# Two 1024-column state adds a step in a selective scan, with the decay shared by ScalarE and GpSimd

## The reference

```
xr, gate = split(x @ W_in.T);  xc = silu(conv4(xr + cond));  xn = layernorm(xc)      # 512 channels
Bm, Cm, dt = split(xn @ W_xproj.T, 3)                                               # 16 each
Ad = 1 - 0.01 * tanh(dt @ W_dt.T + b_dt) * tanh(A_log)
Bd = Bm * min(norm(xn), 1)
h = clip(h * Ad[:, :, None] + Bd[:, :, None] * xn[:, None, :], -10, 10)             # each of 64 positions
y = einsum('bd,bdh->bh', Cm, h)
out = ((y + D * xn) * silu(gate)) @ W_out.T
```

## Time and profile before

| | value |
|---|---|
| median of 3 runs | 1787.09 us |
| profiled execution, its own time | 1789.41 us |
| its span (first to last instruction) | 1787.6 us |
| busy TensorE / VectorE / ScalarE / GpSimd | 1637.6 / 1613.1 / 1296.5 / 621.5 us |
| first instruction of each pass (L2014) | 743.9, 926.2, 1364.9, 1546.9 us |
| mean granted TensorE clock | 0.983 of full |

### The profile page before, as it was taken

The page is one execution under the profiler, slowest core; times in us unless marked ns, Lnnn a source line. Parts: engine busy times, 40 slices in busy tenths (PEclk is TensorE's granted clock), DMA queues, the critical chain, the costliest instruction groups (busy, mean ns, idle before and its releaser), DMA issues. The chain is left out here.

```text
span 1787.6 us, 42368 instructions
## 1 busy us (share of the span) xinstructions
PE 1637.6 (92%) x13764; PEld 703.0 (39%) x13764; DVE 1613.1 (90%) x2452; ACT 1296.5 (73%) x2197; POOL 621.5 (35%) x576
## 2 busy tenths in 40 slices
PE   7999999999999999888888889999997888888898
PEld 3555555555554455322111114444452221111144
DVE  5899999999986999889999998679998899999985
ACT  5655556455546999889999993069998899999920
POOL 0223233232331221365655560002223566555500
PEclk9999999999999999799999999999997999999999
DMA  4000000000001335544555666724445545556668
GB/s 162 2 1 0 1 2 32 2 1 0 1 1 72 139 149 177 191 163 132 182 160 188 219 189 202 239 83 157 144 159 185 179 132 183 155 189 196 189 223 288
DMA packets 126445, 226.56 MB, mean 127 GB/s; under 512 B 35617, under 2 KB 61217, under 8 KB 117537
## 3 DMA queue, kind: packets, MB, share of 16 engines
q1 hardware_dynamic: 125904, 223.30, 38.1%
q10 hardware_dynamic: 432, 1.84, 0.3%
HBM read 141.73 MB, written 83.36 MB: 126 GB/s over the span
## 5 line engine op out<-in xcount | busy, mean ns | idle before, releaser
L1038 ACT ACTIVATE R<-q,Ast 128x512 f32<-128x512 f32 x1008 | 627.0, 709 | 20.3 <-DVE q L2018 15.3
L2018 DVE CUSTOM_DVE_ANT_0 q<-R,PS 128x512 f32<-128x512 f32 x1008 | 617.3, 771 | 15.9 <-ACT R L1038 14.4
L1479 PE MATMUL PS<-xq,Uw 96*128 96x512 bf16 x1024 | 350.0, 396 | 82.3 <-DVE q L2018 71.4
L613 POOL TENSOR_TENSOR Uw<-Ub,rowmask 96x512 bf16<-96x512 bf16 x256 | 335.5, 1346 | 252.1 <-PE PS L1479 252.1
L1492 PE MATMUL PS<-q,Wy 128*32 128x512 f32 x2048 | 284.5, 618 | 0.3
L1479 PEld LDWEIGHTS PS<-xq,Uw 96*128 96x128 bf16 x1024 | 85.6, 97 | 471.1 <-DVE q L2018 399.3
L1152 PE MATMUL PS<-X,Win 128*128 (+1 forms) x456 | 214.5, 607 | 0.1
L1053 PE MATMUL PS<-xn,Wl 128*128 128x512 f32 x384 | 186.5, 609 | 0.8 <-DVE xn L1605 0.7
L1723 DVE SCALAR_TENSOR_TENSOR acc<-xp,Wc,acc 128x512 f32<-128x512 f32 x192 | 134.7, 752 | 2.6
L547 POOL TENSOR_TENSOR ex<-ex,rs 128x1024 f32<-128x1024 f32 x32 | 76.8, 2400 | 164.2 <-DVE rs L1628 164.2
L1152 PEld LDWEIGHTS PS<-X,Win 128*128 128x128 f32 x456 | 82.5, 191 | 92.5 <-issue 91.7
(11 more groups left out here) (159 smaller groups left out, 2491.9 us busy)
## 6 DMA issues: line engine op xcount, KB each, us to landing
xq<-xpart_d SPq DMA_DIRECT2D x384, 192.0 KB
sg_d<-sg SPq DMA_DIRECT2D x16, 1024.0 KB, 5.1
xn_d<-z SPq DMA_DIRECT2D x16, 1024.0 KB, 3.9
y_d<-ys SPq DMA_DIRECT2D x64, 256.0 KB, 3.9
xnp<-xn_d SPq DMA_DIRECT2D x16, 1024.0 KB, 8.4
sgp<-sg_d SPq DMA_DIRECT2D x16, 1024.0 KB, 11.5
xpart_d<-xh SPq DMA_DIRECT2D x16, 512.0 KB, 2.9
xpart_d<-xmi SPq DMA_DIRECT2D x16, 512.0 KB, 3.8
```

The costliest lines, as they stand in the source:

```text
L613: pl.tensor_tensor(Uw[0:XROWS, h, w, :, :, :], Ub[0:XROWS, w, 0:N, ds(s0, CH)].rearrange("p n t -> p t n").unsqueeze(2).broadcast_to([XROW ...
L1038: act.activation(R[:, w, :], q[:, (t + 1) % 2, w, :], ACT.Copy, scale=Ast[:, h, w, t:t + 1]).then_inc(ac_r, 1)
L1479: pe.matmul(PS[:, w, :], Uw[0:XROWS, h, w, t, :, :].rearrange("p b n -> p (b n)"), xq[0:XROWS, hb, w, s8 % XT, :], start=True, stop=True). ...
L2018: v._custom_dve(bass.dve_ops.TENSOR_ADD_SAT, out=q[:, s8 % 2, w, :], in0=R[:, w, :], in1=PS[:, w, :], s0=CLIP, s1=-CLIP).then_inc(dv_q, 1)
```

## The change

- **Two adds a step.** Groups 0 and 1 (p = 0), then 2 and 3 (p = 1) are added in one VectorE instruction of 1024 columns each, over two PSUM banks. `dv_q` counts two a step.
- **The decay is shared.** For each p, ScalarE decays the even group (512 columns) and columns 0 to 95 of the odd one (two instructions); GpSimd decays columns 96 to 511 of the odd group with a product by a broadcast column (`odd_rest`). The add of a pair waits for both (`ac_r`, and the new `pd_r`).
- **The copies of y** (`keep_y`) are moved from VectorE to ScalarE.
- **B is turned.** TensorE transposes `rB` (`turn_b`), VectorE splits it from PSUM, and SyncE stores it in 32-byte pieces into a DRAM image `bdiag_d` of the block-diagonal weights, whose zeros are written once by 12 stores during attention. `Uw` is loaded from it together with x (one more load for each two steps, 72 rows of 2 KB); GpSimd's L613, its row mask, `Ub`, its nine loads a pass and its clearing are gone. The weights have 72 rows in place of 96.
- In pass 0 the last group's middle parts are made on ScalarE, its low parts on GpSimd in halves, each between steps.

The diff, cut to its core:

```diff
+                    for b in range(2):
+                        rows = bdiag_d[ps].rearrange("(j b r) -> j b r", b=2, r=DIAG + N)[:, b, 0:DIAG]
+                        rows = rows.rearrange("j (i t w c n) -> i w c t j n", i=PARTS, t=S, w=QW, c=GB)
+                        for i in range(PARTS):
+                            sp.dma_start(rows[i, ds(w, 1), 0].rearrange("a t j n -> (a t) j n"),
+                                         tvp[b * S:(b + 1) * S, i, :].rearrange("p (j r) -> p j r", r=LANE)[:, :, 0:N]).then_inc(tv_st, 16)
...
                 def load_x(ps, k):
+                    rows = bdiag_d[ps, 0:GB * DIAG].rearrange("(r f) -> r f", f=S * ROW)
+                    sp.dma_start(Uw[0:XROWS, k % XB, :, :, :, :].rearrange("p t w b n -> p (t w b n)"),
+                                 rows[:, k * (XT * ROW):(k + 1) * (XT * ROW)].unsqueeze(0)
+                                 .broadcast_to([PARTS, GB * PARTS, XT * ROW])).then_inc(xq_in[k % XB], 16)
...
+                def odd_rest(pi, c2, s8, p):
+                    h, t = s8 // CH, s8 % CH
+                    if t < 2 and p == 0:
+                        pl.wait_ge(pl_a, pi * CHUNKS + c2 * 2 + h + 1)
+                    pl.wait_ge(dv_q, pi * (2 * S) + c2 * 16 + 2 * s8 + p + 1)
+                    alone(pl)
+                    pl.tensor_tensor(R[:, 2 * p + 1, PART:DI], q[:, (t + 1) % 2, 2 * p + 1, PART:DI],
+                                     Ast[:, h, 2 * p + 1, t:t + 1].broadcast_to([P, DI - PART]), ALU.mult).then_inc(pd_r, 1)
...
-                            for w in range(QW):
-                                act.wait_ge(dv_q, cn * (QW * CH) + QW * t + w + 1)
-                                act.activation(R[:, w, :], q[:, (t + 1) % 2, w, :], ACT.Copy,
-                                               scale=Ast[:, h, w, t:t + 1]).then_inc(ac_r, 1)
+                            for p in range(2):
+                                act.wait_ge(dv_q, cn * (2 * CH) + 2 * t + p + 1)
+                                act.activation(R[:, 2 * p, :], q[:, (t + 1) % 2, 2 * p, :], ACT.Copy,
+                                               scale=Ast[:, h, 2 * p, t:t + 1]).then_inc(ac_r, 1)
+                                act.activation(R[:, 2 * p + 1, 0:PART], q[:, (t + 1) % 2, 2 * p + 1, 0:PART], ACT.Copy,
+                                               scale=Ast[:, h, 2 * p + 1, t:t + 1]).then_inc(ac_r, 1)
+                            if t == 1 and h == 0 and before:
+                                keep_y(pi, c2 * 2 - 1, 1)
+                            if t == 1 and h == 1:
+                                keep_y(pi, c2 * 2, 0)
...
                 body(l * G + G - 2, G - 2, False)
+                pe.wait_ge(tv_s, (l * G + G - 2) * 4 + 2 + TV0)
                 for m in range(DC):
                     variance(l * G + G - 1, m, 6)
...
+                        v.wait_ge(pe_w, pi * (QW * S) + n * QW + 2 * p + 2 + W0)
+                        v.wait_ge(pe_yq, pi * (2 * S) + n * 2 - 4 + p + 1 + USED)
+                        v.wait_ge(pd_r, pi * (2 * (S - 1)) + n * 2 - 2 + p + 1 + READY)
+                        v.wait_ge(ac_r, pi * (4 * (S - 1)) + n * 4 - 4 + 2 * p + 2 + READY)
                         alone(v)
-                        v._custom_dve(bass.dve_ops.TENSOR_ADD_SAT, out=q[:, s8 % 2, w, :], in0=R[:, w, :], in1=PS[:, w, :],
+                        v._custom_dve(bass.dve_ops.TENSOR_ADD_SAT, out=state, in0=R[:, 2 * p:2 * p + 2, :].rearrange("p w c -> p (w c)"), in1=fed,
                                       s0=CLIP, s1=-CLIP).then_inc(dv_q, 1)
```

More of the change, by code:

```diff
@@ L184, in cond_resid_kernel @@
         late = ExitStack()
+        sb("table_gap", [P, TT * DI + P], where=late)
         pass_tables.append(tables(1, late))
@@ L316, in _ @@
             sp.dma_start(fold[:, :], fold_d).then_inc(ld_late, 16)
-            sp.dma_start(rowmask[:, :], rowmask_d).then_inc(ld_late, 16)
             sp.wait_ge(w_mm, G * 2)
+            sp.wait_ge(zero_r, 1)
+            for ps in range(PASSES):
+                rest = bdiag_d[ps, 0:GB * DIAG].rearrange("(p k c) -> p k c", p=P, c=1024)
+                for k in range(GB * DIAG // (P * 1024)):
+                    sp.dma_start(rest[:, k, :], words(zeros).bitcast(bf16)).then_inc(zero_in, 16)
             def load_front(n):
@@ L534, in _ @@
                 pl.memset(eps[:, n:n + 1], value).then_inc(cst, 1)
+            pl.memset(zeros[:, :], 0.0).then_inc(zero_r, 1)
             pl.wait_ge(cst, 5)
@@ new lines, in last_half, with last_group @@
+                def last_half(it, k, b):
+                    if b == 0:
+                        pl.wait_ge(xmi_r, it * TT + k + 1)
+                        alone(pl)
+                    cols = slice(b * (DI // 2), (b + 1) * (DI // 2))
+                    low = pl.tensor_tensor(xlo[:, k, cols], xr1[:, k, cols], xmi[:, k, cols], ALU.subtract)
+                    if b:
+                        low.then_inc(xlo_r, 1)
+                def last_group(n):
+                    it = l * G + G - 1
+                    if n == 20:
+                        pl.wait_ge(xq_st, it * 48 + 48)
+                        alone(pl)
+                    if 20 <= n < 20 + 2 * TT:
+                        last_half(it, (n - 20) // 2, n % 2)
@@ new lines, in eight @@
+                def eight(ps, c2, first=False, last=False, tail=False):
+                    pi = l * PASSES + ps
+                    for s8 in range(8):
+                        for p in range(2):
+                            if not (first and s8 == 0):
+                                odd_rest(pi, c2, s8, p)
+                        if tail:
+                            last_group(c2 * 8 + s8)
+                        if s8 == 0:
+                            if not first:
+                                stage_decay(ps, c2, 1)
+                        elif s8 == 1:
+                            if not first:
+                                stage_outputs(ps, c2, 1)
+                        elif s8 == 4 and not last:
+                            stage_decay(ps, c2 + 1, 0)
+                        elif s8 == 5 and not last:
+                            stage_outputs(ps, c2 + 1, 0)
+                        elif s8 == 5 and ps + 1 < PASSES:
+                            pl.wait_ge(tab_in[1], l * (16 * TABLES) + 16 * TABLES)
+                            alone(pl)
+                            stage_decay(ps + 1, 0, 0, True)
+                            stage_outputs(ps + 1, 0, 0)
+                        elif s8 == 7 and last and ps + 1 < PASSES:
+                            stage_decay(ps + 1, 0, 1, True)
+                            stage_outputs(ps + 1, 0, 1)
@@ L1025, in last_group, with last_middle, keep_y, decayed @@
                         high_part(it, 3, 7)
-                def decayed(pi, c2, first, between=None):
+                def last_middle(n):
+                    for k, at in enumerate((19, 21, 22, 23)):
+                        if n == at:
+                            middle_part(l * G + G - 1, k)
+                def keep_y(pi, ck, h):
+                    act.wait_ge(pe_yq, pi * (2 * S) + ck * (2 * CH) + 2 * CH + USED)
+                    act.wait_ge(y_out[h], pi * (CHUNKS // 2 * 16) + (ck - h) * 8 + 16)
+                    alone(act)
+                    act.activation(ys[:, h, :], PS[:, 4 + h, :], ACT.Copy).then_inc(ac_y, 1)
+                def decayed(pi, c2, first, before, between=None, after=None):
                     for h in range(2):
@@ L1465, in _, with inputs @@
                 alone(pe)
-                def inputs(pi, c2, s8, first=False):
+                def inputs(pi, c2, s8):
                     n = c2 * 8 + s8
-                    cn = pi * CHUNKS + c2 * 2 + s8 // CH
-                    h, t = s8 // CH % 2, s8 % CH
                     hb = s8 // XT % XB
@@ L1503, in _ @@
                                 last_group(c2 * 8 + s8)
-                            inputs(pi, c2, s8 + 1, ps == 0 and c2 == 0)
+                            inputs(pi, c2, s8 + 1)
                             y_of(pi, c2, s8)
@@ L2030, in eight @@
                         step(pi, c2, s8, first)
-                        if s8 == 1 and before:
-                            keep_y(pi, c2 * 2 - 1, 1)
-                        if s8 == 5:
-                            keep_y(pi, c2 * 2, 0)
                 for ps in range(PASSES):
```

261 lines of the change are left out of this document (98 added, 163 removed).

## The result

The changed kernel takes 1899.92 us (median, 1897.1 to 1902.07) against 1787.82 us of the kernel before on the same chip: a ratio of 1.0626, 95% interval [1.0606, 1.0646]. It is slower by 112 us, where 1781 us were forecast. One profiled execution further down, that of e2_three_loads, took 3036 us where its four others took 1824 to 1840, so its trace is not used.

What follows compares the result with a forecast made beforehand. VectorE's instruction rate was taken as the bound, ScalarE close behind. Steady steps +2, last group -10 and scan's start +2 gave -6 us, 1781 on the median of 1787.1; range 1762 to 1812, the forecast's own 1765 to 1783.

Steps and rivals of the forecast that it cites:

- the 204 steady steps: All scan steps but 26 in each pass 0: 2.55 us a step against 2.54, +2 us in all.
- The queue is late: Rival: B's small stores, x and weights together, 25% more bytes; a few us dearer, in the slow cases; chance 0.06.
- Up to 3 us a layer late. I take +1 for each layer in all: Scan's start: later variance matmuls and B's 32-byte stores on SyncE's queue; +1 us a layer, +2 in the sum.
- 72 rows of weights in place of 96 move the same 512 columns: nothing.: TensorE's input products in the scan: fewer rows of weights would change the time by nothing.
- As the order there is the same, it stays: TensorE's clock at the scan's start, 743.9 to 769.3 us: would stay at 0.70.
- 2.55 a step: Steady scan step: a pair's longer ring of 2.52 us plus 0.03 for disturbances, against 2.54 before.
- both rings: A pair's add, decay and hand-off back to its next add: 2.50 us through ScalarE, 2.52 through GpSimd.
- A gap of about 0.3 us before each first add: Expected VectorE profile sign: an idle gap after each two adds, ended by ScalarE's 96-column decay or by GpSimd.
- The last group, -5.1 a layer: Work slipped into pass 0's steps: -5.1 us a layer, -10 in all, with -2.5 from VectorE's 0.29 us of room.
- Adds as the bound: Rival: rings overlap more, TensorE's ring and VectorE set 2.28 us a step; 1726 us; chance 0.12.
- GpSimd's ring: Rival: product and hand-off for the odd group's 416 columns take longer, 2.67 us a step; 1807 us; chance 0.30.
- TensorE waiting for DMA at L1479's place: Profile sign that would show the forecast wrong, pointing to a late queue.

Runs made afterwards that it cites:

- e2_three_loads: The changed kernel with the weights in three loads of the same 24 rows, not one with 3 repeats outermost; 1830.14 us, ratio 1.0188.
- a1c: The changed kernel with weights loaded only for each layer's first four slots, each waited for by itself, then reused stale; 1806.87 us, ratio 1.0098.
- h1: The changed kernel with input products over 96 rows, the added rows being ones against zero weights loaded once a layer; 1895.57 us, ratio 1.0582.
- g2: The changed kernel's arithmetic (two adds, shared decay) on h3's transfers, with products over 96 rows; 1795.30 us, ratio 1.0032.
- f1: The changed kernel with one x load, three weights loads, four 512-column adds, ScalarE decaying three groups, GpSimd the fourth; 1790.96 us, ratio 1.0010.
- h2: f1 with its products over 96 rows, the added rows being ones against zero weights loaded once a layer; 1775.49 us, ratio 0.9907.
- f2: f1 with the products of x's lowest part left out, so 48 rows are loaded and multiplied; 2041.47 us, ratio 1.1408.
- h3: f2 with its products over 96 rows, 48 of them ones against zero weights; 1759.34 us, ratio 0.9818.

## Why the prediction was wrong

- **What failed: the 204 steady steps have no term for their loads, and "The queue is late ... a few us dearer, in the slow cases" was all the price they got.** The sum takes (2.55 - 2.54) x 204 = +2 us for these steps, from the engines' rings alone. But the weights' loads come with each load of x, in every second step. I took 25% more bytes as a small thing and did not ask which DMA engines the new load lies on. Measured: 43.6 and 34.2 us in the two second passes (after against a1c), 0.8 and 10.3 in the first ones, 89 in all; by the medians 93 of the 112 us. The shape of the load was there to be read beforehand, with the rule cited above: 3 repeats outermost is 48 KB on each of three engines, beside the 48 KB of x that they had in any case.
- **"Up to 3 us a layer late. I take +1 for each layer in all": not far off.** This term was for the scan's start. The first add of the first layer comes 0.9 us later than before (744.8 against 743.9), the stretch to the second layer's first add is 2.1 us longer (274.9 against 272.8).
- **What failed, smaller: "72 rows of weights in place of 96 move the same 512 columns: nothing."** Their duration is the same (0.60 us for two of them with 72 rows as with 96 in h1). But with 72 rows the first passes have less of the clock (0.86 in a1c's first one, 0.94 in g2's) and are longer: a1c against g2 is 190.5 and 184.6 against 181.9 and 180.0, 13 us together. These two differ in their loads also; f1 and h2 differ in the rows and their filling alone, and h2's first passes are 3.0 and 4.6 us shorter. While the three engines set the pace these us do not show on top (h1). "As the order there is the same, it stays", said of the clock at the start, failed with it: in the first 25.4 us of the scan the granted clock is 0.63 in the changed kernel and 0.50 in a1c, where it was 0.70.
- **2.55 a step: right; how it is made up: not quite.** In each of g2's second passes 61 of 62 steps take 2.5 to 2.6 us, 2.547 in the mean, and these passes are 166.9 against 165.9, +1.0 each, where I had +2 for all. Add 1.22, product 0.88 (0.89), ScalarE's rest 0.36. But both rings are 2.55 long in a clean step, not 2.50 and 2.52, because starts and hand-offs are 0.01 to 0.03 us longer each, and the copies and `Wy` disturb nothing, where I had 0.03 a step. The two small errors cancel, which is luck. "A gap of about 0.3 us before each first add" was 0.17.
- **The last group, -5.1 a layer: right in sign, too large.** g2 measures -0.4 and -2.0 us for the whole first passes. I had given 2.5 of it to the 0.29 us of room that VectorE has in a step; but a ring of 2.55 in a step of 2.55 has no room on any engine. In a1c, between 808.52 and 812.12, a step with one slipped-in copy on ScalarE takes 3.60 us: the copy (0.60) starts only at 810.35, when TensorE's product for it is there, and the decays of the next pair stand behind it.
- **The rivals.** "Adds as the bound" and "GpSimd's ring" were about the arithmetic, and the arithmetic was as forecast. The queue was the right place, but it had a chance of 0.06 and no number beyond a few us, for another reason than the one that the runs showed. In the first rival, the 14 of "1787 - 8 - 14 = 1765" is worked out nowhere, though 1765 is the lower end of the forecast. Of what the profile after would show wrong, "TensorE waiting for DMA at L1479's place" is what came.

Had the transfers been what I took them for, an estimate from g2 is 1795.3 less 4.3 us (its fill rows: the first add at 745.5 against 744.8, and 278.5 against 274.9), 1791: no change, not -6.

## What to carry to other kernels

Before a load is added, ask of each transfer which dimension is outermost and over how many DMA engines that spreads it, and add up the bytes of the fullest engine; the mean DMA share says nothing about it. Here a mean share of 0.65 beside waits for loads was the sign that few engines were full. And a product over fewer rows was no cheaper here, but it could cost the clock: here rows of ones against weights of zero, which change no result, were worth 282 us (f2 to h3), 15 us by the medians (f1 to h2), and nothing that can be told from noise where late loads set the pace (after to h1).
